# Two gated layers with attention and experts on one core: three elementwise steps change engine, and every engine's order is rewritten

## The reference, cut to what matters

```python
def _layernorm(x, eps=1e-05):
    return (x - mean(x)) / sqrt(var(x) + eps)

# x, ctx: (32, 128, 256) f32
r = scan(0.9 * r + ctx * ctx)                        # along the 128 positions
x = x + tanh(g_xattn[0]) * _layernorm(x) * r         # norm A, gives x1
y = _layernorm(x)                                    # norm B
lw = softmax(l2norm(y @ Wp.T + bp) @ l2norm(sim) * scale)      # 4 adapters, ranks 1, 2, 4, 8
x = x + tanh(g_ffn[0]) * (y @ W.T + lw[top1] * (y @ Wd[top1].T) @ Wu[top1].T)    # gives x2
q, k, v = _layernorm(x) @ Wq, ctx @ Wk, ctx @ Wv     # norm C, 16 heads of 16
p = sigmoid(where(mask, q @ k.T / 4, -1e30))
x = x + tanh(g_xattn[1]) * (p @ v) @ Wo              # gives x3
y = _layernorm(x)                                    # norm E
x = x + tanh(g_ffn[1]) * top2_of_8_experts(y)        # gelu(y @ w_in + b_in) @ w_out + b_out
```

## Time and profile before

| | |
|---|---|
| median of 3 runs | 478.92 us (477.81 to 485.43) |
| the profiled execution's own time | 478.9 us |
| span of its instructions | 478.9 us |
| mean granted TensorE clock | 0.96 |

### The profile page before, as it was taken

The page is one execution under the profiler, slowest core; times in us unless marked ns, Lnnn a source line. Parts: engine busy times, 40 slices in busy tenths (PEclk is TensorE's granted clock), DMA queues, the critical chain, the costliest instruction groups (busy, mean ns, idle before and its releaser), DMA issues.

```text
span 478.9 us, 13099 instructions
## 1 busy us (share of the span) xinstructions
PE 396.5 (83%) x4092; PEld 309.2 (65%) x4092; DVE 370.2 (77%) x1416; ACT 330.9 (69%) x671; POOL 251.4 (53%) x313
## 2 busy tenths in 40 slices
PE   2758899998999989998899887789568898989950
PEld 1446667776776777676677765478457797777740
DVE  2788888998988889898888785368556566789993
ACT  2755788898889889998888775576616564655640
POOL 1621212545553464637453556678876676766760
PEclk9988999999999999999999999889969999999995
DMA  7336686664575555876454665525353559397975
GB/s 231 90 111 178 181 215 177 183 194 133 166 227 182 162 174 161 244 178 209 144 170 125 220 189 146 166 67 151 90 157 103 165 162 335 101 351 244 330 262 201
DMA packets 69501, 87.12 MB, mean 182 GB/s; under 512 B 9485, under 2 KB 55290, under 8 KB 69306
## 3 DMA queue, kind: packets, MB, share of 16 engines
q1 hardware_dynamic: 60074, 65.81, 47.4%
q0 software_dynamic: 6816, 18.65, 10.5%
q10 hardware_dynamic: 2544, 1.81, 1.2%
HBM read 51.07 MB, written 35.18 MB: 180 GB/s over the span
## 4 chain that ended last, share of the span: by engine, by line
PE 46%; DVE 14%; issue 13%; POOL 11%; ACT 8%; DMA 6%; another core or an unknown queue 1%; ACTq 1%; DVEq 0%; POOLq 0%; SPq 0%
PE ps_J L1654 13%; PE ps_F L1654 6%; PE ps_O L1768 5%; PE ps_T L1663 5%; PE ps_S L1755 4%; POOL store_x L765 4%; POOL pause_t L782 3%; PE ps_S L1654 3%; DMA store_y<-y_out,y_row 2%; POOL store_y L771 2%; PE ps_R L1693 2%; DVE y_out L2938 2%; PE ps_O L1779 2%; PE ps_G L1654 2%; DMA temp_t<-in_temp 2%
## 5 line engine op out<-in xcount | busy, mean ns | idle before, releaser
L771 POOL DMA_INDIRECT store_y<-y_out,y_row x78 | 78.4, 1005 | 41.6 <-DVE y_out L2938 29.5
L765 POOL DMA_INDIRECT store_x<-xn_E,slot_u x64 | 68.8, 1076 | 27.1 <-DVE slot_u L2637 16.9
L1093 ACT ACTIVATE prob<-ps_S 128x512 f32<-128x512 f32 x128 | 72.4, 594 | 12.0 <-PE ps_S L1755 7.6
L1755 PE MATMUL ps_S<-q_stack,k_stack 128*128 128x256 f16 x256 | 44.5, 276 | 5.6 <-issue 3.5
L2926 DVE TENSOR_TENSOR h_lo<-h_f,h_hi 128x512 f16<-128x512 f32 x39 | 26.9, 689 | 24.5 <-ACT h_hi L1177 19.6
L1654 PE MATMUL ps_J<-wout_hi,h_hi 128*128 x112 | 31.2, 278 | 15.2 <-DVE y_out L2938 12.9
L1768 PE MATMUL ps_O<-prob,v_wide 128*32 128x128 f32 x1024 | 41.0, 279 | 1.1 <-ACT prob L1093 0.9
L1169 ACT ACTIVATE h_f<-ps_F,bin_t 128x256 f32<-128x256 f32 x56 | 23.5, 471 | 25.9 <-PE ps_F L1654 20.1
L1654 PE MATMUL ps_F<-xb_hi,win_hi 128*128 128x256 f16 x112 | 31.8, 284 | 4.1 <-DVE xb_lo L2907 2.7
L1779 PE MATMUL ps_O<-wo_t,av 128*128 128x256 f32 x128 | 32.8, 401 | 2.3 <-ACT av L1121 1.6
L751 POOL TENSOR_TENSOR rstd_C<-var_C,minus_half 128x2 f32<-128x2 f32 x16 | 12.2, 761 | 40.3 <-DVE var_C L2416 40.3
(11 more groups left out here) (302 smaller groups left out, 1410.6 us busy)
## 6 DMA issues: line engine op xcount, KB each, us to landing
parts_scratch<-parts SPq DMA_DIRECT2D x32, 256.0 KB
k_stack<-parts_scratch SPq DMA_DIRECT2D x64, 128.0 KB
q_stack<-parts_scratch SPq DMA_DIRECT2D x128, 64.0 KB
xb<-store_x SPq DMA_DIRECT2D x30, 257.0 KB
y_got<-store_y SPq DMA_DIRECT2D x14, 512.0 KB
c_in<-in_ctx SPq DMA_DIRECT2D x16, 256.0 KB
x_in<-in_x SPq DMA_DIRECT2D x16, 256.0 KB
store_x<-zeros SPq DMA_DIRECT2D x15, 257.0 KB, 4.8
```

What stands on the lines that cost most here:

```text
L765: pool.indirect_dma_start(store_x, bass.IndirectOffsetOnAxis(slot_u[q][:, at:at + 1], 0), xn_e[q][:, at, :], None).then_inc(s_scat[q], 16)
L771: pool.indirect_dma_start(store_y, bass.IndirectOffsetOnAxis(y_row[n][:, b:b + 1], 0), y_out[n][:, b, :], None).then_inc(s_y_kept[n], 16)
L1093: act.activation(prob[m % PROBS][:, 2 * n:2 * n + 2, :, :], bank_s[n], ACT.Sigmoid, scale=float(HD) ** -0.5).then_inc(s_prob[n], 1)
L1755: ins = pe.matmul(bank_s[n][:, g % 2, :, :], k_stack[q][:, g, k, cut], q_stack[q][:, :, g, k, cut], start=True, stop=True)
```

## The change

What it does:

- **Norm A.** The ACTIVATEs of `gained` and VectorE's `shifts_a` are gone. `moves` is now two instructions, (x - mean) times scan, which need the statistics but neither rstd nor the gate. `make_x1` is two instructions, moved times ln_gain plus x. The semaphores moved and x1 count two to a pair.
- **Norms B and C.** The ACTIVATEs and `shifts` are gone. VectorE writes (x - mean) times rstd with two TENSOR_SCALAR of 128x256 each. Norm E stays as it was.
- **Orders.** Every engine's list is rewritten and the expert stage's loops are unrolled. The number of every call is the same (39 long and 32 short pauses among them); they stand elsewhere. Many pauses between scatters of the pairs are gone and stand in a row in other places. Around the last pairs' scatters GpSimd goes from keep_block(0, 0) to (1, 1) without pause, then scatter(14, 2), one pause, keep_block(2, 0) to (3, 1); scatter(15, 3) and (15, 0) stand behind keep_block(8, 1) and scatter(15, 2) behind keep_block(10, 0). On ScalarE `squared(0)` stands ahead of `gates_tanh` (and of the issue of the DMA small_bias). On VectorE `final_plan` ends two tiles later, between take_rows(12) and take_rows(13) and ahead of add_bias(10) (before: ahead of add_bias(8)); ten `add_pair` instead of twelve stand ahead of add_bias(38), the others behind it. `gate_ratios` stands between gelu(7) and hidden_hi(7). On TensorE scan(0) stands ahead of the first transposes, and some neighbouring tiles' transposes stand together. On SyncE the first loads are context 0, x 1, x 0, context 1.

The diff, cut to its core:

```diff
@@ ScalarE
-            def gained(p):
-                q = p % 2
-                act.wait_ge(s_shift["A"], p + 1)
-                need(act, s_x2, p - 1)
-                for b in range(2):
-                    act.activation(x1[q][:, b, :], x_in[q][:, b, :], ACT.Identity, bias=shift["A"][q][:, b:b + 1],
-                                   scale=ln_gain[q][:, b:b + 1]).then_inc(s_xn["A"], 1)
-
-            def normed_b(p):
...
-            def normed_c(p):
...
@@ TensorE
-                need(pe, s_moved, p)
+                need(pe, s_moved, 2 * p)
@@ VectorE
-            def shifts_a(p):
+            def moves(p):
                 q = p % 2
-                dve.wait_ge(s_gain, p + 1)
-                dve.scalar_tensor_tensor(out=shift["A"][q][:, :], in0=mv["A"][q][:, :, 0], scalar=-1.0,
-                                         in1=ln_gain[q][:, :], op0=ALU.mult, op1=ALU.mult).then_inc(s_shift["A"], 1)
-
-            def moves(p):
                 dve.wait_ge(s_scan, p + 1)
-                dve.wait_ge(s_xn["A"], 2 * p + 2)
-                need(dve, s_x1, p)
-                dve.tensor_tensor(moved[:, :, :], x1[p % 2][:, :, :], bank_r, ALU.mult).then_inc(s_moved, 1)
+                dve.wait_ge(s_aggr["A"], 2 * p + 2)
+                need(dve, s_x1, 2 * p)
+                for b in range(2):
+                    dve.scalar_tensor_tensor(out=moved[:, b, :], in0=x_in[q][:, b, :], scalar=mv["A"][q][:, b, 0:1],
+                                             in1=bank_r[:, b, :], op0=ALU.subtract, op1=ALU.mult).then_inc(s_moved, 1)
 
             def make_x1(p):
                 q = p % 2
-                dve.wait_ge(s_moved, p + 1)
-                dve.tensor_tensor(x1[q][:, :, :], moved[:, :, :], x_in[q][:, :, :], ALU.add).then_inc(s_x1, 1)
+                dve.wait_ge(s_moved, 2 * p + 2)
+                dve.wait_ge(s_gain, p + 1)
+                need(dve, s_x2, p - 1)
+                for b in range(2):
+                    dve.scalar_tensor_tensor(out=x1[q][:, b, :], in0=moved[:, b, :], scalar=ln_gain[q][:, b:b + 1],
+                                             in1=x_in[q][:, b, :], op0=ALU.mult, op1=ALU.add).then_inc(s_x1, 1)
+
+            def normed(k, p, src):
+                dve.wait_ge(s_rstd[k], p + 1)
+                need(dve, s_t[k], p)
+                for b in range(2):
+                    dve.tensor_scalar(xn[k][:, b, :], src(b), mv[k][p % 2][:, b, 0:1], rstd[k][p % 2][:, b:b + 1],
+                                      ALU.subtract, ALU.mult).then_inc(s_xn[k], 1)
...
@@ GpSimd
-            scatter(0, 3)
-            long_pause()
             scatter(0, 0)
-            long_pause()
+            inverse_root("C", 4)
             scatter(0, 1)
-            inverse_root("C", 4)
             scatter(0, 2)
...
@@ SyncE
+            load_ctx(0)
+            load_x(1)
             load_x(0)
+            load_ctx(1)
             load_weights(s_wkv, C_K, C_Q)
...
```

More of the change, by code:

```diff
@@ L984, in _ @@
[L984 to L996 removed]
+            keep_block(4, 0)
+            keep_block(4, 1)
+            keep_block(5, 0)
+            keep_block(5, 1)
+            keep_block(6, 0)
@@ L3985, in _ @@
-            for n in range(TILES + 1 - ADD_AT, NP):
-                add_pair(n)
+            take_rows(13)
+            add_bias(10)
+            hidden_lo(11)
+            copy_lo(13)
+            take_rows(14)
+            hidden_lo(12)
+            add_bias(11)
+            copy_lo(14)
+            hidden_lo(13)
+            add_bias(12)
+            copy_lo(15)
+            hidden_lo(14)
+            take_rows(15)
+            add_bias(13)
+            copy_lo(16)
+            take_rows(16)
@@ new lines, in _ @@
+            hidden_lo(24)
+            next(gates)
+            add_bias(23)
+            hidden_lo(25)
+            take_rows(24)
+            copy_lo(27)
+            add_bias(24)
+            hidden_lo(26)
+            next(gates)
+            next(gates)
+            copy_lo(28)
+            take_rows(25)
+            add_bias(25)
+            copy_lo(29)
+            take_rows(26)
+            take_rows(27)
+            take_rows(28)
+            hidden_lo(27)
+            add_bias(26)
+            add_pair(0)
```

2360 lines of the change are left out of this document (1394 added, 966 removed).

## The result

The changed kernel takes 485.25 us (median of 20 executions, 481.49 to 489.05) against 481.21 us for the kernel before beside it (20 executions, 476.05 to 488.4). The ratio is 1.010 with a 95% interval of 1.008 to 1.013: slower by 1%, where 465.8 us and a gain of 2.7% were forecast, outside the range of 454 to 483. The profiled execution took 484.62 us with a span of 482.8, against a span of 478.9 before. A ratio leaves out executions over 1.5% above the fastest of their kernel, a median beside it is that of all executions, so the two can differ by more than the interval.

A forecast was written before the change was run, and what follows sets the result against it. TensorE was taken to bound the pairs, VectorE and ScalarE close behind, with a stall at 337 to 370 us and VectorE leading from 420. +3 - 2.3 - 8 - 3 - 2.8 = -13.1 took 478.9 to 465.8 us; range 454 to 483.

The forecast's parts named there:

- The moved work, by pair: Pairs: VectorE gains 1.25 us a pair, ScalarE falls from 14.6 to 11.0; taken as +0.2 a pair, +3 us.
- rival D: Pairs, 40 to 280 us: VectorE becomes the bound, all added time (1.25 to 1.6 a pair) counts; 488.8 us, chance 0.12.
- The start: Start to x1 of pair 0: first halves need neither gate nor rstd, x1 earlier; -2.3 us, between 0 and -4.
- The rule: VectorE in a two-port mode and GpSimd lock each other out; named as speaking against the forecast, priced as rival E.
- rival E: Normed steps: GpSimd holds them 0.23 us on average, 64 steps, +15 us; 480.8 us, chance 0.07.
- The stall: 337 to 370 us: VectorE's 6.04 us wait for tile 3's scatter goes; -8 us, between 0 and -14.
- The signals: Expert stage: new places keep scatters off the ends of TensorE's matmuls, fewer late signals; -3 us, between +3 and -8.
- Rival C: Behind the pairs: stall moves, scatters meet signals elsewhere, only -3 of the -8 and -3 together; 473.8 us, chance 0.16.
- The last tiles: From 420 us: two add_pairs go behind add_bias(38), into a wait that hides them; -2.8 us, between 0 and -3.4.
- B: Pairs get faster too, ScalarE having been late for TensorE: -7 in place of +3, x2 steps below 16.4; 455.8 us, chance 0.18.

The follow-up runs named there:

- e2: Kernel before with the change of engine alone, in its own orders: ACTIVATEs and shift calls out, normed steps of B and C on VectorE; 501.77 us, ratio 1.026.
- e12: Kernel before with keep_block(3, 0) and (3, 1) moved ahead of the last pair's four scatters, pauses as they were; 467.24 us, ratio 0.996.
- e13: Kernel before without its long pauses from scatter(14, 3) to keep_block(3, 1), order unchanged; 462.31 us against 468.55, ratio 0.987.
- e4: Changed kernel with a long pause between any two adjacent scatters from keep_block(0, 0) to keep_block(12, 1); 493.32 us, ratio 1.006 against the kernel before.
- e7: Changed kernel with every engine's calls in the order of the kernel before from tile 24 on; 487.16 us, ratio 0.988 against the kernel before.
- e8: Changed kernel with every engine's calls in the order of the kernel before from tile 4 on; 482.27 us, ratio 0.975 against the kernel before.
- e15: Changed kernel with the old order from tile 4 on for SyncE, ScalarE, TensorE and VectorE, GpSimd keeping its new one; 480.62 us, ratio 0.983 against before.
- e1: Changed kernel with GpSimd's four fills of query and value tiles moved ahead of its first inverse root; 487.48 us, ratio 0.986 against the kernel before.
- e17: The kernel of e1 again, beside the changed kernel; 483.46 us, ratio 0.992 against the kernel before.

## Why the prediction was wrong, by its own steps

The sum was -13.1 us and the spans differ by +3.9, so it missed by 17.0: +5.2 at the start, -8.7 in the pairs, +20.5 behind them. The steps that decided are the stall, the signals and the last tiles, all priced as gains from what the new lists take away. That the pairs gained was not foreseen and hides a part of the miss.

- **The moved work, by pair.** "I take +0.2 a pair, +3 us": measured -5.7. VectorE's added work was right in size (1.25 forecast, 1.0 measured, with a normed step of 0.41 for 0.33) and TensorE waited for it hardly more than before (from 40 to 280 us 1.8 us ahead of the transposes of xn_C, 1.1 before). What I priced was a list in which only the engine changes; e2 shows that this costs 0.7 us a pair, above the 0.2 taken and about half of rival D's 1.25. The orders were not costed as a part of their own. The step that failed is reading a change of engine and of order as one.
- **The start.** "-2.3 us", measured +2.9. The forecast part came (x1 1.7 us earlier). Missing was the hold of the normed steps by the fills, 3.9 us. I had the row for it, a ln_gain held by such a fill for 0.13 us, and the Trainium skill's rule; I dismissed both because the median of 16 ln_gains was unmoved. That reading was right for pows and scatters (20 of the 64 normed steps started under a scatter and took 0.39 to 0.59 us) and wrong for fills: a median says nothing of the one place where a long GpSimd instruction stands on the path. In the new list the first normed step stood exactly beside 4.6 us of fills.
- **The rule.** The Trainium skill (SBUF — State Buffer, "SBUF: two separate sides") has GpSimd and VectorE exclude each other for a whole instruction when VectorE is in a two-port mode, or has two inputs in SBUF while GpSimd's instruction reads SBUF. The trace agrees at the start, in both directions (4.64 us for 0.73 beside fills, and an inverse root of 1.82 for 0.71 beside w_lo, which reads two tensors in SBUF). It agrees only in part beyond it: GpSimd is busy half of the time in the pairs, and of 64 normed steps all but three ended within 0.6 us. By the rule as I had priced it (rival E, +15 us) the pairs would have been slower; they were faster.
- **The stall.** "I take -8": measured +4.5 over tiles 0 to 16. The wait of 6.04 us did go, and the gap from tile 6 to tile 7 fell from 11.7 to 5.1 us; but tiles 0 to 6 took 5.5 us longer and tiles 7 to 16 5.6. The step that failed is that nothing else would fill the room. The 1.84 us a step was also miscounted: six scatters from 334.36 to 345.40 are five steps, 2.2 us each. e12 and e13 show the two things that I took as one: the order only passes the wait on (-1.3 us by the medians), the pauses are what it costs (-6.2 us where no signal is late). Where signals are late, part of the time went into them instead: the idle time behind late ones rose by 7.9 us from 310 to 385 us, and e4, whose pauses took it away there, had tile 7 7.3 us earlier. How much of the rest is the order of the four other lists and how much late signals stays open.
- **The signals.** "-3, between +3 and -8": the idle time behind late ones rose from 25.5 to 31.2 us, +5.7 summed over the engines, not all of it on the path. The sign was forecast from what the change is for; no row supported it. Rival C called them "a matter of tenths of a microsecond" against its own row of 2.55 us, and it was priced as a loss of 8 us of gain, never as a loss against before.
- **The last tiles.** "-2.8 us": measured +5.4 from tile 16 to 38. I costed the two add_pairs that left the stretch and nothing of the other engines' lists, which run neighbouring tiles together, nor SyncE's, which puts the last three loads 27 us later. e7, e8 and e15 show the cost: 7 to 12 us from tile 4 on. That VectorE's busy time in the stretch fell was forecast, that this would shorten it was not followed by a bound for what comes next.

The rivals: none of them was it. The pairs went B's way (x2 steps of 16.3, under its sign of 16.4), though by the orders and the engine together and not by the engine; the stage went C's way and worse, the start E's in one place. The common fault is that edits were priced by what they take away, at the place that they touch, and the rewritten lists around them were taken as neutral.

## What to carry to other kernels

A rewritten order is a part of the change with a price of its own, of either sign: price it stretch by stretch, and keep a bound above zero where no row says that it helps. Before a step moves to VectorE, look for GpSimd's longest instructions beside its new place, and put fills where GpSimd waits anyway; here four lines were worth 4 to 5 us. In the expert stage the lists in which each tile's steps keep one even sequence beat those that run neighbouring tiles together by 7 to 12 us; that they absorb late events better is my reading and was not shown. A kernel tuned on one chip should be timed on a second. Before counting late events in a trace, check that the waiting instruction was late as well.

## What the runs showed of the hardware

- A TENSOR_SCALAR of 128x256 f32 on VectorE (0.41 us) is held by a fill on GpSimd (0.95 or 1.8 us): two of them took 4.64 us beside three fills and 0.73 without, one took 3.64 us in e2. Beside scatters and pows they took 0.39 to 0.59 us.
- The other way round, a pow of 128x2 on GpSimd took 1.82 us beside a TENSOR_TENSOR of 128x1024 with two inputs in SBUF (1.21 us), again 1.81 in e1 and e17, and 0.71 without.
- TensorE's signals arrived late on some chips and not on two others, with the same kernels. Engines started behind a signal over 0.2 us late in 22 to 45 places of a run on the former and in none on the latter. By the wider count it is 73 to 104 of 551 signals, by 135 to 212 us in all, against 1 to 4. Most late ones end under a scatter of GpSimd's (57 of the 80 in the first trace of before, 69 of the 94 after), where 29 to 30% of all signals do. Long pauses between the scatters took away all places from 310 to 385 us (e4). What differs between the chips was not found.
- The kernel before takes 468.6 and 469.1 us on the chips without late signals, 4% less than the 486.6 to 488.4 on the three others.
- The same pair of kernels gives 1.010 in the first measurement and 0.999 and 1.000 on two chips, with intervals of 0.3 to 0.4% to either side: the ratio differs by more than an interval taken in one place.
